# Projections, output projection, shift rows and bias in 64-column matmuls, in another order of one window pair's work

## What is computed

```
xn  = group_norm(x, 32 groups, no scale or shift)
xn  = roll(xn, (-3, -3)); q, k, v = split(xn @ w_qkv.T)
# windows of 7 x 7 = 49 positions, 12 heads of 32 channels
dots = q @ k.T * 32**-0.5 + pos_emb[relative position] + mask(last row, last column of windows)
o    = softmax(dots) @ v
y    = x + roll(o @ w_out.T + b_out, (3, 3))
```

## Time and profile before

| | us |
|---|---|
| median of 3 runs | 4586.72 |
| lowest, highest | 4585.05, 4587.34 |
| the profiled execution | 4584.81 |
| its span, first to last instruction | 4583.0 |

### The profile page before, as it was taken

One profiled execution on the slowest core, in us unless ns is written; L12 is line 12 of the kernel. 1 busy time (PEld: TensorE's weight loads), 2 busy tenths in 40 slices (PEclk: granted clock), 3 DMA queues, 4 the chain that ended last, 5 costly groups with the idle time before them and its releaser, 6 DMA issues.

```text
span 4583.0 us, 164167 instructions
## 1 busy us (share of the span) xinstructions
PE 4390.2 (96%) x64360; PEld 2981.1 (65%) x64360; DVE 4046.9 (88%) x9283; ACT 2275.8 (50%) x4225; POOL 2282.0 (50%) x1933
## 2 busy tenths in 40 slices
PE   3999999999999999999999999999999999999998
PEld 1666666666666666666666666666666666666665
DVE  5898898989989998898989989899898988999886
ACT  0555555455554545555555455555555555555554
POOL 1455445455554554555455455545545545554454
PEclk9999999999999999999999999999999999999999
DMA  4344344334343433443343443334434433434332
GB/s 122 103 106 107 99 107 116 94 108 114 99 109 105 108 104 103 107 109 98 105 119 95 108 112 100 107 106 108 105 97 109 115 95 107 115 98 108 98 95 60
DMA packets 231099, 478.93 MB, mean 105 GB/s; under 512 B 39009, under 2 KB 140898, under 8 KB 222818
## 3 DMA queue, kind: packets, MB, share of 16 engines
q1 hardware_dynamic: 230338, 468.43, 38.6%
HBM read 159.99 MB, written 77.07 MB: 52 GB/s over the span
## 4 chain that ended last, share of the span: by engine, by line
PE 74%; DVE 16%; issue 7%; ACT 2%; SPq 0%; DMA 0%; POOL 0%; DVEq 0%; POOLq 0%; ACTq 0%
PE ps_pj L1087 24%; PE ps_pj L1083 13%; PE ps_post L1181 13%; PE ps_post L1172 5%; PE ps_sa L1121 4%; PE ps_st L1121 3%; PE ps_pv L1165 2%; DVE mt L928 2%; PE ps_st L1150 2%; PE ps_pv L1164 2%; PE ps_pv L1163 2%; DVE atl L907 2%; DVE mw L917 2%; PE ps_pj L1071 2%; DVE st L701 1%
## 5 line engine op out<-in xcount | busy, mean ns | idle before, releaser
L554 POOL TENSOR_TENSOR pl<-pf,ph 64x588 f16<-64x588 f32 x512 | 732.1, 1430 | 1622.3 <-ACT ph L669 1595.0
L599 ACT ACTIVATE qk<-ps_pj 128x392 f16<-128x392 f32 x768 | 381.9, 497 | 978.7 <-PE ps_pj L1087 978.7
L669 ACT ACTIVATE ph<-ps_st,sc 64x588 f16<-64x588 f32 x1024 | 772.5, 754 | 6.5
L1087 PE MATMUL ps_pj<-xh,wh 128*128 128x392 f16 x2304 | 765.2, 332 | 5.5 <-POOL xl L529 4.6
L1087 PE MATMUL ps_pj<-xh,wl 128*128 128x392 f16 x2304 | 764.6, 332 | 0.0
L1087 PE MATMUL ps_pj<-xl,wh 128*128 128x392 f16 x2304 | 764.5, 332 | 0.0
L575 POOL TENSOR_TENSOR rb<-tq,cst 128x588 bf16<-128x588 bf16 x512 | 701.2, 1370 | 48.1 <-ACT tq L658 8.1
L529 POOL TENSOR_TENSOR xl<-xn,xh 128x392 f16<-128x392 f32 x384 | 343.4, 909 | 599.0 <-DVE vl L860 293.0
L865 DVE TENSOR_TENSOR qk<-ps_pj,qk 128x392 f16<-128x392 f32 x768 | 432.8, 564 | 228.3 <-ACT qk L599 225.4
L664 ACT ACTIVATE pf<-ps_st,sc 128x588 f32<-128x588 f32 x512 | 384.7, 751 | 359.1 <-PE ps_st L1121 359.1
L953 DVE TENSOR_TENSOR pl<-pf,ph 64x588 f16<-64x588 f32 x512 | 543.4, 1061 | 0.5 <-ACT ph L669 0.5
(11 more groups left out here) (107 smaller groups left out, 9582.0 us busy)
## 6 DMA issues: line engine op xcount, KB each, us to landing
stack<-qk SPq DMA_DIRECT2D x1536, 147.0 KB
sx<-in_x SPq DMA_DIRECT2D x66, 1176.0 KB, 7.0
xs<-in_x SPq DMA_DIRECT2D x384, 84.0 KB
out<-xb SPq DMA_DIRECT2D x384, 84.0 KB
xs<-in_x SPq DMA_DIRECT2D x384, 63.0 KB
out<-xb SPq DMA_DIRECT2D x384, 63.0 KB
xs<-in_x SPq DMA_DIRECT2D x128, 66.0 KB
out<-xb SPq DMA_DIRECT2D x128, 66.0 KB
```

The source lines that it names most:

```text
L554: nc.gpsimd.tensor_tensor(pl[PAD:, :, PAD:PAD + N], pf[PAD:, :, :], ph[PAD:, :, PAD:PAD + N], ALU.subtract).then_inc(s_pl[1], 1)
L669: e = nc.scalar.activation(ph[rows, :, w * PAD:w * PAD + N].rearrange("p (a h) n -> p a h n", a=2), ps_st[rows, :, 0:HH * N].rearrange("p ...
L1087: m = mm(ps_pj[bank][:, 0:RT].rearrange("p (w n) -> p w n", w=NW), wa[:, c, o:o + 128], xa[:, b, c, :, 0:N], **on)
```

## The change

- `project_unit`, `project_out`, `shift_rows` and the bias matmul are each written as two matmuls of 64 (for the output projection 64 and 34) stationary columns, one after the other, with the same moving operand and the PSUM partitions 0 to 63 and 64 up (`SIDES`).
- TensorE's step becomes: scores(t), units 1, attend(t-2), transpose_attended(t-3), units 2, transposed_scores(t-1), shift_rows(t), units 3, project_out(t-3).
- `FILL`: in k = 1 and 5 x0 stands before q2 and x1 before k2.
- DVE: `attended_low` goes behind `normalize`; `split_probabilities` goes ahead of the third units, `output` behind them, to the step's end. ACT: `attended_high` goes behind the first units.
- SP: instead of a row's 10 loads at once, the loads of one pair in each step (`reload`, for the pair three steps on), behind the stack copies and ahead of the store.

```diff
+SIDES = (slice(0, PAD), slice(PAD, 2 * PAD))
...
-        ([("k", 1)], [("q", 2), ("x", 0)], [("k", 2), ("x", 1)]),
+        ([("k", 1)], [("x", 0), ("q", 2)], [("x", 1), ("k", 2)]),
...
+            def reload(tk, j):
+                odd, p = j // 4, j % 4
+                if tk.last:
+                    return
+                reach(s_xb, 8 * tk.n + j + 1)
+                if p == 0:
+                    reach(s_pj, ROW_FIRST + 13 if tk.first and odd else
+                          (ROW_FIRST if tk.first else unit_count(tk.back, 4 * odd + X_TICK[2], "x", 2)))
+                move_row(sp, x, xs[:, odd, p, :], s_load[odd], p, True, rows_of(ahead(tk), odd))
...
-                    if p == 0 and not tk.last:
-
-                        reach(s_xb, 8 * n + 4 * odd + 4)
...
-                        load_row(ahead(tk), odd)
...
+                    if not (tk.last and k + LEAD >= 8):
+                        reload(tk if k + LEAD < 8 else ahead(tk), (k + LEAD) % 8)
                     if not (tk.first and k < 3):
                         store(t - 3, tk, k - 3)
...
# project_unit
+                        for s, half in enumerate(SIDES):
+                            if kind == "v":
+                                m = mm(ps_pj[bank][half, 0:C], xa[:, b, c, 2 * i + s, :], wa[:, c, 2 * C:3 * C],
+                                       skip_group_check=True, **on)
+                            else:
+                                o = (C if kind == "k" else 0) + i * 128 + s * PAD
+                                m = mm(ps_pj[bank][half, 0:RT].rearrange("p (w n) -> p w n", w=NW), wa[:, c, o:o + PAD],
+                                       xa[:, b, c, :, 0:N], skip_group_check=True, **on)
...
# shift_rows
-                    m = mm(rows_out[:, hh, :], mt[:, hh, :], eb[:, :], start=True, stop=True)
+                    for half in SIDES:
+                        m = mm(rows_out[half, hh, :], mt[:, hh, half], eb[:, :], start=True, stop=True)
...
# transposed_scores
-                    mm(out, bt[:, kind, :], rb[:, hh, :, :].rearrange("p h n -> p (h n)"),
-                       start=True, stop=False, skip_group_check=True)
+                    for half in SIDES:
+                        mm(ps_st[half, hh, 0:HH * N], bt[:, kind, half], rb[:, hh, :, :].rearrange("p h n -> p (h n)"),
+                           start=True, stop=False, skip_group_check=True)
...
# project_out
-                        m = mm(ps_post[0:PT, 0:C], a[:, c, :], w[:, c, :], start=c == 0 and n_ == 0,
-                               stop=c == KC - 1 and n_ == 2)
+                        for part in (slice(0, PAD), slice(PAD, PT)):
+                            m = mm(ps_post[part, 0:C], a[:, c, part], w[:, c, :], start=c == 0 and n_ == 0,
+                                   stop=c == KC - 1 and n_ == 2, skip_group_check=True)
```

More of the change, by code:

```diff
@@ L543, in _ @@
             pool.wait_ge(s_pjr, 14)
-            for j in range(3):
+            for j in range(LEAD):
                 residual(j, 0, j)
@@ L567, in step @@
                         x_lows(tk, k)
-                    if not (tk.last and k + 3 >= 8):
-                        residual(t + 3, n, k + 3)
+                    if not (tk.last and k + LEAD >= 8):
+                        residual(t + LEAD, n, k + LEAD)
                     if not (tk.first and k < 1):
@@ L637, in step @@
                     t = 8 * tk.n + k
+                    if not (tk.last and k >= 4):
+                        units(tk, k, 0)
                     if not (tk.first and k < 3):
@@ L975, in step @@
                         units(tk, k, 0)
-                    if not (tk.first and k < 3):
-                        attended_low(t - 3)
                     if tk.finishes and k == 4:
@@ L989, in step @@
                         normalize(t - 2)
+                    if not (tk.first and k < 3):
+                        attended_low(t - 3)
                     if not (tk.last and k >= 4):
@@ L997, in step @@
                     between(5)
+                    if not (tk.first and k < 1):
+                        split_probabilities(t - 1)
+                    between(5)
+                    if not (tk.last and k >= 4):
+                        units(tk, k, 2)
                     if not (tk.first and k < 3):
                         output(t - 3, k - 3)
-                    between(5)
-                    if not (tk.first and k < 1):
-                        split_probabilities(t - 1)
-                    if not (tk.last and k >= 4):
-                        units(tk, k, 2)
                     between()
@@ L1191, in step @@
                     scores(t, tk, k)
-                    if not (tk.first and k < 3):
-                        transpose_attended(t - 3, k - 3 + 8)
                     if not (tk.last and k >= 4):
@@ L1197, in step @@
                         attend(t - 2, *back(tk, k, 2))
+                    if not (tk.first and k < 3):
+                        transpose_attended(t - 3, k - 3 + 8)
                     if not (tk.last and k >= 4):
@@ L1201, in step @@
                         transposed_scores(t - 1, *back(tk, k, 1))
-                    if not (tk.first and k < 3):
-                        project_out(t - 3)
                     shift_rows(t)
@@ L1206, in step @@
                         units(tk, k, 2)
+                    if not (tk.first and k < 3):
+                        project_out(t - 3)
             def image(m):
@@ L1217, in _ @@
             end = 8 * (LAST + 1)
+            attend(end - 2, Tick(B - 1, PARTS - 1), 6)
             transpose_attended(end - 3, 5)
-            attend(end - 2, Tick(B - 1, PARTS - 1), 6)
             transposed_scores(end - 1, Tick(B - 1, PARTS - 1), 7)
```

18 lines of the change are left out of this document (5 added, 13 removed).

## The result

The kernel after takes **4460.11 us** (median of 4 runs, 4448.47 to 4469.95), the kernel before 4586.86 (4 runs, 4585.05 to 4587.34): a ratio of 0.9723, 95% interval 0.970 to 0.9747. Predicted were 4475 us, from 4365 to 4610. The execution profiled took 4448.47 us, its span is 4446.7. So the total came out nearly as forecast. Its parts did not, as the following sections show.

A forecast was written before the change was run, and what follows sets the result against it. TensorE was taken to bound, DVE close behind. From 4584.8 us, -3.2 saved on width changes plus waits (3.5 - 2.0) gave -1.7 us a Tick, -109 over 64 Ticks: 4476, median 4478, said as 4475; range 4365 to 4610.

The forecast's parts named there:

- TensorE bounds, DVE follows: Whole kernel: TensorE's own pace is 67.6 of 69.6 us a Tick; DVE close behind with 7.9 us of work a pair.
- Price of a change of width: TensorE between wide and narrow matmuls: 0.09 to 0.10 us going in, 0.11 going back, 0.66 us a pair before.
- Narrow pairs cost nothing: The 252 wide matmuls a Tick that become pairs: each pair keeps 0.17 (0.16) us; bias and shift-row pairs cost nothing.
- Saved 3.2 us a Tick: TensorE's width changes fall from 0.66 to 0.26 us a pair: 0.40 saved, 3.2 a Tick, 205 us in all.
- new waits of 3.5 us a Tick against old ones of 2.0: TensorE's waits for DVE: shift rows, x1 and 0.6 for statistics make 3.5 us a Tick; the old 2.0 go.
- 3.5 plus L: DVE's chain to the shift rows ends 3.5 us after the scores plus DVE's lateness L, put at 0.2 to 1.2.
- DVE keeps pace: Rival: DVE's chain ends before POOL's `xl` begins, new waits 1.3 us a Tick, total near 4335 to 4400; chance 0.22.
- The statistics' share, 0.6 us a Tick: Extra waits from the Tick that works out an image's statistics, shared out over all Ticks: 0.6 us each.
- the first rival: DVE's lateness stays at 0.2, new waits 1.3 us a Tick: -250 us, near 4335 to 4400; chance 0.22.
- The price of the second rival: DVE loop takes the bound: lateness 1.5 in all steps, waits 9.2 us a Tick, 4640 or more; chance 0.14.
- Loads: nothing: SP's loads of x by pair, not 10 at a time, last pair asked for at the same point: no effect.
- Stack copies "just fit": SP's stack copies begin near 2.3 us into step 2, land at 13.5 to 14.5; the scores need them at 14.8.

The follow-up runs named there:

- narrow_only: Kernel before with all four narrowings into 64-column pairs and nothing moved (orders, units' table and loads as before): 4620.1 us, ratio 1.0075.
- stack_first: Kernel after with SP issuing the stack copies of k = 2 and 6 ahead of the store of the pair before: 4471.5 us, ratio 0.9747.
- wide_out: Kernel after with the output projection alone wide again, 9 matmuls instead of 9 pairs: 4544.7 us, ratio 0.9911.
- order_only: Kernel after with all four narrowings taken back to wide matmuls; order, units' table and loads stay changed: 4559.5 us, ratio 0.9939.
- al_early: Kernel after with DVE's remainder of the attended values put back ahead of the maxima: 4819.4 us, ratio 1.0519.
- out_middle: Kernel after with the output projection back between transposed scores and shift rows, and DVE's output addition ahead of the split: 4591.9 us, ratio 1.0019.
- roots_late: Kernel after with statistics units ahead of the split and the inverse root's twelve operations spread over k = 6, 7 and next 0, 1: 4398.4 us.
- roots_idle: Kernel after with statistics units ahead of the split and inverse-root operations only at k = 5 (five) and k = 7 (seven): 4352.6 us, ratio 0.9495.

## Why the prediction was right in its total, and where not

- **TensorE bounds, DVE follows.** Held where it was followed: the gains and losses traced here are TensorE's pace or a wait of TensorE's. Some are not traced (half of what narrow_only missed, TensorE's idle time in stack_first).
- **Price of a change of width.** Held: 0.09 to 0.10 us going in, 0.10 to 0.11 coming out (and 0.04 more for a projection behind it), measured at the places where it went and, in wide_out, where it came back.
- **Narrow pairs cost nothing.** Held: 0.170 us a pair. The two shift-row pairs and their way to the next unit take 0.06 us in all (2029.10 to 2029.16), 30 ns a pair. The Trainium skill, page "TensorE: Matmul & The Clock Gate", section "LDWEIGHTS (loading the stationary operand)", says that a load takes its columns / 1.2 ns; two loads of 64 would by that take 107 ns, an estimate of mine. This trace contradicts it.
- **Saved 3.2 us a Tick.** Only 1.7 came (order_only against after): 0.38, 0.04, 0.34 and 0.11 at k = 0 to 3, where my count gives 0.45, 0.24, 0.45 and 0.45. The waits of 0.19 at k = 1 and 0.21 at k = 3 explain 0.4 of the missing 0.72, the projection's 0.04, which order_only has already saved, 0.16 in the four steps; the last 0.16 stays open.
- **The term that failed: new waits of 3.5 us a Tick against old ones of 2.0.** It was wrong twice. In an ordinary Tick the new waits are about 0.8 (predicted 2.9: shift rows 0.3, 1.0, 0.1 and 0.4, x1 0.8 and 0.3; found 0 and 0.21, twice each, x1 none, but k2 behind it 0.19). The old ones that went were about 2.0, not 1.5: order_only's Tick is 2.3 shorter, with every change of width still in it but the projection's 0.3. The places on TensorE were right, 4.15 us for 4.20 at k = 2 and 5.8 at k = 1. Wrong was DVE's side, "3.5 plus L": at k = 3 of after the maxima are ready here:

```profile
2033.64 0.75 DVE L912 TENSOR_TENSOR lg<-ps_sa,bc 128x588 f32<-128x588 f32 x1
...
2035.99 0.18 DVE L944 TENSOR_TENSOR mt<-mw,mt 128x24 bf16<-128x24 f32 x1
```

  The scores began at 2032.14, so the chain ends 4.03 us behind them: L = 0.5, where the wait of 1.0 that I wrote down means 1.3, more than my own upper end of 1.2. I had carried the split over at its old 1.06 us and added 0.9 for contention, though the move itself decides who meets whom at the port. That the collisions go is half of the rival "DVE keeps pace", and its reason held too: at k = 2 the chain ended at 2028.50, and POOL's `xl` began at 2029.38.
- **The statistics' share, 0.6 us a Tick.** It should have been 2.3: 9.7 us in each of 15 Ticks, 145 us against 38 (the one shown has 9.3). I shared it out as a remainder and did not walk through the step in which DVE has two more long operations ahead of the logits and TensorE's bank hangs on a unit behind the split. With ordinary Ticks alone the first rival would have been right, at its lower end: -4.0 x 64 = -256 us, some 4330.
- So two errors of opposite sign met. My -3.2 + 2.9 - 1.5 = -1.8 us for an ordinary Tick was -4.0, and my 0.1 for the statistics, spread over all Ticks, was (9.7 - 2.4) x 15 / 64 = 1.7. Only together do they come near the forecast: -2.2 by the pace of the scores, where I had -1.7. That the total came within 15 us of the forecast is luck.
- **The price of the second rival was added up wrong.** +4.0 x 64 is 256 us, so 9.2 us of waits a Tick would give some 4840, not 4640. al_early, with a Tick of 71.0, shows how dear such waits are: 4819.
- **Loads: nothing.** Right against the kernel before and misleading all the same: without them the unit order moved by the same change costs 158 us. I had checked whether the loads are asked for earlier or later, not whether their consumer moves.
- **Stack copies "just fit".** Held, just: 14 rows of some 127 waited, 0.4 us each. They began at 2.76 us instead of my 2.3; moving them 2.1 us earlier brings nothing.
- **No rival for pieces.** I priced the change as a whole. Each of the two edits that take a piece of the order back costs more than the whole brings (out_middle +132, al_early +359 us on after): both lie on the one cycle between the two engines, and either can bind alone. Of the other pieces that is not shown.

## What to carry over

Grouping matmuls of one width pays about 0.2 us for each wide block that no longer stands alone among narrow ones, but only if no wait of TensorE's lies next behind it, so change the order and the widths together and judge neither alone. Where a step is moved forward on one engine, look up what feeds it (a load, a bank, an operand of the slower engine), and walk once through the rare step that carries extra work: here 15 of 64 Ticks took back 110 of 256 us. A short operation of VectorE is best put where GpSimd is idle, or behind everything that TensorE waits for: with four of them at k = 6, one of 0.19 us held for 1.25 beside a long one of GpSimd's, the next step took 4 us longer than with none.

## What the runs showed of the hardware that was not expected

- Half clock behind waits: in after the granted clock is 0.50 for 3 us at k = 5 in 13 of the 15 statistics' Ticks, in the one shown behind waits of 1.04 and 1.96 us within 7 us of each other; the matmuls then start 0.33 us apart, not 0.17. In roots_late it is 0.51 from 1913 to 1916, behind the wait of 2.62 us, and so in 14 of its 15 Ticks; behind the wait of 2.67 us at k = 7 of after it came in only 5 of 15, and not in the one shown. So the length of the wait alone does not decide it. The mean granted clock of after's execution is 0.989, of roots_idle's and of before's 0.998, and these have no such run of waits.
- narrow_only has more time in waits than before and the clock of before (0.998): its waits are at most 1.0 us each. al_early, with waits of 1.1 to 2.7, has 0.982.
- An operation of DVE held by POOL's took 1.25 us instead of 0.19, and the new order, which parts such neighbours, took 403 of 4047 us of busy time off DVE for the same instructions.
